# Cross-attention block on one Trainium2 core: denominators' sums over keys moved from TensorE to accumulating transfers and VectorE, the residual moved to transfers

## The chip, the cores and the metric

The kernel runs on one NeuronCore of a Trainium2 chip. The metric is device time in microseconds (us) for one execution, the median of a few runs; lower is better. All arithmetic is float32.

## The reference

Queries are 4096 rows of `x` (512 wide), keys and values come from 3202 rows of a context, there are 16 heads of 32. What matters, cut from the reference:

```python
xq  = _ada_ln(x_q,  t_vec, Wss_q,  bss_q)      # layer norm, then scale and shift from silu(t_vec)
xkv = _ada_ln(x_kv, t_vec, Wss_kv, bss_kv)
q  = (xq @ Wq + bq).reshape(B, Lq, nh, dh)
kv = (xkv @ Wkv + bkv).reshape(B, Lkv, 2, nh, dh)
k, v = kv[:, :, 0], kv[:, :, 1]
scores = jnp.einsum('bqhd,bkhd->bhqk', q, k) / jnp.sqrt(jnp.float32(dh))
attn = jax.nn.softmax(scores, axis=-1)
out = jnp.einsum('bhqk,bkhd->bqhd', attn, v).reshape(B, Lq, H)
return x_q + (out @ Wp + bp)
```

## The kernel before, in words

**Stages.** A first stage of about 230 us normalises the context, projects keys and values and stores them in DRAM; it also normalises the rows of `x` and projects the queries of the first block. Then comes the attention, on which all that follows bears. A check at the end (a flag computed from the largest denominator and reciprocal) can start an exact second pass; with these inputs it isn't taken.

**Units and tiles.** The 4096 queries are 8 blocks (`b`) of 512. The 16 heads are 4 groups (`g`) of 4 heads. One block with one group is a unit (`u = 4*b + g`, 32 units). Each unit goes over 25 tiles (`t`) of 128 keys; the last two keys of the 3202 are the "tail" and are treated apart. In a tile TensorE makes the scores of the next tile (`scores`, L1152, keys on the partitions), ScalarE takes exp of them in two instructions of 128x1024 (`weights`, L1411) into one of five buffers `pt`, and TensorE multiplies the values with them (`weigh`, L1164), accumulating in a PSUM bank over the unit. VectorE adds up the `pt` buffers (L1738): even and odd tiles go to two accumulators `acc` and `odd`, 23 additions of 128x2048 in a unit, and a 24th (L1747) joins the two. ScalarE may not write a `pt` buffer again before TensorE and VectorE have both read it, five tiles later.

**Side work.** TensorE has room for one small extra step behind `weigh` in each tile, written out by hand: `first_side` for `g == 0` and `later_side` for the others. The steps are parts of the query projection of the next block (L1184), of the output projection of the block before (L1222), the scores of the tail (L1207), and the denominators (`denominators`, L1195): in tiles 5 and 6 of a unit, TensorE multiplies the joined accumulator of the unit before with ones, which sums over the 128 partitions, that is over keys. All these results land in the one bank that isn't accumulating; ScalarE takes them out (`take_queries` L1420, `take_output` L1440, `take_denominators` L1427), and a `jobs` list orders them.

**From denominators to outputs.** SP (the engine that issues nearly all transfers, in program order, each behind its own waits) stores the denominators in DRAM (`store_l`, L771). Once per block it loads them, with the tail's weights, as a 128x64 tile (`load_l`, L799), VectorE adds and inverts them (`invert`, L1642 to L1649), SP stores the reciprocals and loads them back, each copied to 32 partitions (`store_r`, `load_r`), and VectorE multiplies (`divide`, L1671, four instructions of 128x512). The products feed the output projection. VectorE adds the bias to the rows of `x` (`add_bias`, L1678) and these to each output tile (`add_residual`, L1684); SP stores it (`store_y`, L832). The last unit alone sums its denominators by TensorE with the tail included, and turns them with VectorE transposes (L1754 to L1762).

**Other waits.** SP also loads the keys and values of the next unit in five parts (`load_kv`, L750 and L751, after `pv_done` of the same part), and the tail's weights copied to 32 partitions (`load_tail`, L788). POOL (GpSimd) does nothing in the attention. TensorE waits at a side step for `job_taken` of the job before (`free`), and at `denominators` for `p_added`.

Of the kernel before, what the change touches and what calls it, by code (L numbers as in the profile page):

```python
# [5 lines left out]
P = 128  # L6
F32 = mybir.dt.float32
I32 = mybir.dt.int32
ALU = mybir.AluOpType
# [7 lines left out]
NH = 16  # L17
# [4 lines left out]
def cross_attention(nc, x, ctx, cond, Wq, bq, Wkv, bkv, Wp, bp, Wss_q, bss_q, Wss_kv, bss_kv, out):  # L22
    _, LQ, H = x.shape
    LKV = ctx.shape[1]
    DH = H // NH
# [52 lines left out]
    def attention():  # L78
        with ExitStack() as st:
# [47 lines left out]
            l_blk = sb("l_blk", [P, QB * NH // P])  # L127
            l_t = sb("l_t", [P, 2, QB * NH // P])
            l_a = sb("l_a", [P, QB * NH // P])
            l_c = sb("l_c", [P, QB * NH // P])  # L130
            r_blk = sb("r_blk", [P, QB * NH // P])
            r_few = sb("r_few", [P, QB // DH])
            l_tops = sb("l_tops", [P, 2, NB + 1])
# [12 lines left out]
            acc = [part(5 + i).rearrange("p (h q) -> p h q", h=HG) for i in range(2)]  # L146
            odd = [part(i).rearrange("p (h q) -> p h q", h=HG) for i in (7, 12)]
            acc2 = odd[0]
            on = part(8).rearrange("p (g q) -> p g q", g=NG)
            r_b = part(9).rearrange("p (g q) -> p g q", g=NG)  # L150
            xy = [part(i).rearrange("p (j f) -> p j f", j=TPB) for i in (10, 13)]
# [55 lines left out]
            l_out = sem("l_out")  # L207
# [3 lines left out]
            l_in = sem("l_in")  # L211
            l_step = sem("l_step")
            r_done = sem("r_done")
            r_out = sem("r_out")
            r_in = sem("r_in")
            on_ready = sem("on_ready")
            xy_in = sem("xy_in")
            xy_ready = sem("xy_ready")
            y_added = sem("y_added")
            y_out = [sem(f"y_out{j}") for j in range(TPB)]  # L220
            turned = sem("turned")
# [64 lines left out]
            def schedule():  # L286
                jobs = []
                for b in range(NB):
                    for g in range(NG):
                        u = NG * b + g  # L290
                        if g == 0:
                            if b > 0:
                                jobs.append(("q", b, 3, 0))
                                jobs.append(("l", u - 1))
                                jobs.extend(("q", b, 3, i) for i in range(1, q_parts(3)))
                            jobs.append(("p", b))
                            if b > 0:
                                jobs.extend(("y", b - 1, 0, i) for i in range(2))
                        else:
                            if b > 0:  # L300
                                jobs.append(("y", b - 1, g, 0))
                            jobs.append(("l", u - 1))
                            if b > 0:
                                jobs.extend(("y", b - 1, g, i) for i in (1, 2))
                            if b + 1 < NB:
                                jobs.extend(("q", b + 1, g - 1, i) for i in range(2))
# [18 lines left out]
            def added(u):  # L325

                return ADDS * u
# [140 lines left out]
            def exact_pool(pool):  # L468
                for j in range(TPB):
                    pool.wait_ge(y_out[j], 16 * NB)  # L470
# [214 lines left out]
            with nc.Block() as block:  # L685
                @block.sync
                def _(sp):
# [80 lines left out]
                    def store_l(u):  # L768
                        b, g = divmod(u, NG)
                        sp.wait_ge(job_taken, JOB["l", u] + 1)  # L770
                        sp.dma_start(l_dram[g * HG:(g + 1) * HG, b * QB:(b + 1) * QB],  # L771
                                     l_sb[0:P:DH, :]).then_inc(l_out, 16)
# [18 lines left out]
                    def load_l(b, heads):  # L791

                        cols = slice(b * QB, (b + 1) * QB)
                        rows = heads * P // NH
                        sp.wait_ge(l_out, 16 * (NG * b + heads // HG))
                        sp.wait_ge(pt_out, 16 * NG * (b + 1))
                        if b > 0:
                            sp.wait_ge(l_step, 4 * b)
                        sp.dma_start(l_blk[0:rows, :], l_dram[0:heads, cols].rearrange("h (a q) -> h a q", a=P // NH)  # L799
                                     ).then_inc(l_in, 16)  # L800
                        for k in range(TAIL):
                            src = pt_dram[:, cols].rearrange("(h k) q -> k h q", k=TAIL)[k, 0:heads, :]
                            sp.dma_start(l_t[0:rows, k, :], src.rearrange("h (a q) -> h a q", a=P // NH)
                                         ).then_inc(l_in, 16)

                    def store_r(b, heads):
                        rows = heads * P // NH
                        sp.wait_ge(r_done, b + 1)
                        sp.dma_start(r_dram[0:heads, b * QB:(b + 1) * QB].rearrange("h (a q) -> h a q", a=P // NH),
                                     r_blk[0:rows, :]).then_inc(r_out, 16)  # L810

                    def load_r(b, heads):
                        groups = heads // HG
                        sp.wait_ge(r_out, 16 * (b + 1))
                        if b == 0:
                            sp.wait_ge(xs_out[4], 16)
                        if b > 0:
                            sp.wait_ge(on_ready, NG * b)
                        for h in range(HG):
# [992 lines left out]
```

## Time and profile before

| | |
|---|---|
| Median of 3 runs (lowest to highest) | 2140.96 us (2140.28 to 2142.82) |
| Profiled execution, its own time | 2138.16 us |
| Profiled execution, its span | 2136.4 us |
| Granted TensorE clock, mean | 0.999 of full speed |
| Busy share: TensorE / VectorE / ScalarE / GpSimd | 99% / 90% / 84% / 1% |
| DMA, mean rate over the span | 99 GB/s |

How to read it: PE is TensorE's matmuls, PEld its weight loads (which overlap PE), DVE VectorE, ACT ScalarE, POOL GpSimd, SP the engine that issues transfers. "L1164" is line 1164 of the kernel before. A float32 matmul shows as two records. Matmuls are pipelined and their ends are modelled, so the distance from one `weigh` to the next says more of a tile's length than busy time does. A timeline row gives start, duration, engine, line, operation, output and input, and a count if equal instructions are merged; a bracket is the idle time ahead and who ended it.

### The profile page before, as it was taken

What the parts mean: (1) busy time and instruction counts of PE and PEld (TensorE: products, weight loads), DVE (VectorE), ACT (ScalarE), POOL (GpSimd) and SP (SyncE); (2) the same over time, 40 slices, a digit from 0 to 9 for tenths busy, and PEclk for the clock granted to TensorE, in tenths of its full rate; (3) what the DMA queues carried; (4) which work ended last, traced back from release to release, by engine and by line L of the source; (5) the groups of instructions that cost most, each with busy time, mean ns of one, the idle gap of its engine ahead of it and who ended that gap; (6) DMA issues with size and microseconds to landing.
All of it is one profiled execution on the core that took longest, in us unless ns stands there. A gap on an engine that the chain in (4) does not pass through costs nothing.

```text
span 2136.4 us, 56258 instructions
## 1 busy us (share of the span) xinstructions
PE 2114.3 (99%) x25036; PEld 604.5 (28%) x25036; DVE 1923.6 (90%) x1197; ACT 1802.1 (84%) x1923; POOL 17.3 (1%) x28
## 2 busy tenths in 40 slices
PE   7999999999999999999999999999999999999998
PEld 3444322222222222222222222222222222222222
DVE  2435799999999999999999999999999999999998
ACT  1212799999999999999999999999999999999995
POOL 0001000000000000000000000000000000000000
PEclk9999999999999999999999999999999999999999
DMA  9346534223422343223422342223432332232321
GB/s 314 115 161 235 148 86 97 77 80 92 118 75 77 95 102 86 67 80 92 121 71 82 89 122 71 78 79 89 110 83 71 101 95 78 70 84 78 97 55 52
DMA packets 202260, 212.35 MB, mean 99 GB/s; under 512 B 18838, under 2 KB 136222, under 8 KB 202012
## 3 DMA queue, kind: packets, MB, share of 16 engines
q1 hardware_dynamic: 199468, 208.16, 35.1%
q8 instruction: 198, 3.24, 0.6%
q10 hardware_dynamic: 2544, 0.53, 0.1%
q14 instruction: 50, 0.41, 0.1%
HBM read 170.38 MB, written 38.26 MB: 98 GB/s over the span
## 4 chain that ended last, share of the span: by engine, by line
PE 98%; DVE 1%; DMA 0%; issue 0%; ACT 0%; POOL 0%; SPq 0%; DVEq 0%
PE bank L1152 40%; PE bank L1164 37%; PE bank L1222 5%; PE bank L1184 5%; PE bank L1056 4%; PE bank L1067 4%; PE bank L1195 1%; PE bank L1280 1%; PE bank L1036 0%; DVE stats L1507 0%; PE bank L1207 0%; DMA arena<-in_L_xcond_Wss_kv_dram 0%; DVE arena L1525 0%; PE bank L1001 0%; PE bank L1097 0%
## 5 line engine op out<-in xcount | busy, mean ns | idle before, releaser
L1411 ACT ACTIVATE arena<-bank,shift 128x1024 f32<-128x1024 f32 x1600 | 1692.5, 1114 | 132.9 <-PE bank L1152 131.4
L1738 DVE TENSOR_TENSOR arena<-arena 128x2048 f32<-128x2048 f32 x736 | 1641.3, 2283 | 60.7 <-ACT arena L1411 59.0
L1152 PE MATMUL bank<-qs,ks 32*64 32x512 f32 x12800 | 918.2, 613 | 1.2 <-ACT arena L1369 0.7
L1164 PE MATMUL bank<-arena,vg 128*32 128x512 f32 x6400 | 852.3, 605 | 1.2 <-ACT arena L1411 1.2
L1164 PEld LDWEIGHTS bank<-arena,vg 128*32 128x32 f32 x6400 | 125.9, 108 | 650.5 <-ACT arena L1411 650.5
L1152 PEld LDWEIGHTS bank<-qs,ks 32*64 32x64 f32 x12800 | 205.0, 129 | 366.4 <-ACT arena L1411 227.0
L1222 PE MATMUL bank<-wp,arena 128*32 128x168 f32 (+2 forms) x2464 | 153.6, 321 | 0.0
L1184 PE MATMUL bank<-xt,wq 128*32 128x256 f32 (+2 forms) x2016 | 143.0, 355 | 0.0
L1222 PEld LDWEIGHTS bank<-wp,arena 128*32 128x32 f32 x2464 | 80.1, 110 | 184.3 <-issue 165.4
L1369 ACT ACTIVATE arena<-bank,bk_c 128x512 f32<-128x512 f32 (+1 forms) x28 | 17.9, 642 | 128.6 <-PE bank L1056 120.5
L1184 PEld LDWEIGHTS bank<-xt,wq 128*32 128x32 f32 x2016 | 65.5, 110 | 150.8 <-issue 132.8
L1056 PE MATMUL bank<-arena 128*128 128x512 f32 (+1 forms) x224 | 90.8, 549 | 1.2 <-ACT arena L1346 1.2
L1067 PE MATMUL bank<-arena 128*128 128x512 f32 x200 | 90.2, 594 | 0.6 <-DVE arena L1587 0.6
L1587 DVE TENSOR_TENSOR arena<-bank,bv_b 128x512 f32<-128x512 f32 x25 | 16.9, 688 | 77.6 <-PE bank L1067 77.6
L1747 DVE TENSOR_TENSOR arena<-arena 128x2048 f32<-128x2048 f32 x32 | 73.4, 2292 | 1.1
L1056 PEld LDWEIGHTS bank<-arena 128*128 128x128 f32 x224 | 39.7, 190 | 44.6 <-issue 43.9
L1067 PEld LDWEIGHTS bank<-arena 128*128 128x128 f32 x200 | 37.7, 190 | 47.3 <-issue 45.7
L1525 DVE TENSOR_SCALAR arena<-arena,aggr,rstd 128x512 f32<-128x512 f32 x54 | 25.9, 542 | 20.8 <-POOL rstd L960 20.8
L1346 ACT ACTIVATE arena<-bank,mod 128x512 f32<-128x512 f32 (+1 forms) x28 | 18.6, 746 | 29.7 <-PE bank L1036 15.7
L1507 DVE BATCH_NORM_STATS2 stats<-arena 128x6 f32<-128x512 f32 x54 | 33.6, 680 | 6.2 <-DMA arena<-in_ctx_dram 6.1
L1195 PE MATMUL bank<-arena,ones 128*32 128x256 f32 x496 | 38.1, 379 | 0.0
L1671 DVE TENSOR_TENSOR arena<-o_all,arena 128x512 f32<-128x512 f32 x31 | 19.4, 686 | 11.2 <-DMA arena<-l_recip 11.2
(97 smaller groups left out, 384.9 us busy)
## 6 DMA issues: line engine op xcount, KB each, us to landing
ks<-k_full SPq DMA_DIRECT2D x160, 320.0 KB, 3.1
vg<-v_full SPq DMA_DIRECT2D x160, 320.0 KB, 3.8
p_b<-p_tails SPq DMA_DIRECT2D x128, 128.0 KB, 4.2
arena<-in_x_dram SPq DMA_DIRECT2D x15, 1024.0 KB, 9.8
q_full<-qs SPq DMA_DIRECT2D x32, 256.0 KB, 2.0
out_dram<-arena SPq DMA_DIRECT2D x32, 256.0 KB, 2.5
x_normal<-arena SPq DMA_DIRECT2D x7, 1024.0 KB, 7.6
xin<-x_normal SPq DMA_DIRECT2D x28, 256.0 KB, 10.1
```

The costliest lines, as they stand in the source:

```text
L1056: mm = nc.tensor.matmul(bank[:, 4 + 2 * (n % 2), 0:width], w[:, k, m * P:(m + 1) * P], src[:, k, 0:width], start=(k == 0), stop=(k == FT - 1))
L1067: mm = nc.tensor.matmul(bank[:, 5 + 2 * (n % 2), :], ct[c % 2][:, k, j * P:(j + 1) * P], wkv[:, k, H:2 * H], start=(k == 0), stop=(k == FT ...
L1152: mm = nc.tensor.matmul(bank[out, 2 * (i % RING) + h % 2, :], ks[rows_of(h), keys], qs[rows_of(h), g, :], start=True, stop=True)
L1164: mm = nc.tensor.matmul(bank[rows_of(h), o_bank(u), :], vg[:, t, rows_of(h)], pt[t % PR][:, h, :], start=(t == 0), stop=False, skip_group_ ...
L1184: mm = nc.tensor.matmul(bank[rows_of(c), side_bank(u), cols], wq[:, k, col:col + DH], xt[:, k, cols], start=(k == 0), stop=(k == FT - 1), ...
L1195: mm = nc.tensor.matmul(bank[rows_of(h), side_bank(u), halves_of(half)], ones[:, :], acc[of % 2][:, h, halves_of(half)], start=True, stop= ...
L1222: mm = nc.tensor.matmul(bank[rows_of(c), side_bank(u), cols], on[:, k, row:row + DH], wp[:, k, cols], start=(k == 0), stop=(k == NG - 1), ...
L1411: nc.scalar.activation(pt[t % PR][:, 2 * pair:2 * pair + 2, :], bank[:, first:first + 2, :], ACT.Exp, scale=SCALE, bias=shift[:, g:g + 1]) ...
L1507: i = nc.vector.bn_stats(stats[:, j, :], src[:, j, :])
L1525: return nc.vector.tensor_scalar(to, rows, aggr[:, j, 0:1], rstd[:, j:j + 1], ALU.subtract, ALU.mult)
L1738: nc.vector.tensor_tensor(a[:, :, :], (pt[t - 1] if k <= 2 else a)[:, :, :], pt[t % PR][:, :, :], ALU.add).then_inc(p_added, 1)
L1747: nc.vector.tensor_tensor(sums[0][:, :, :], sums[0][:, :, :], sums[1][:, :, :], ALU.add).then_inc(p_added, 1)
```

## The change

TensorE's `denominators`, ScalarE's `take_denominators` and VectorE's joining addition go, except for the last unit. In their place, for each unit but the last: SP copies partitions 0 to 31 of both accumulators into a tile `folds` whose rows belong to head `h` (`first_folds`, four transfers of 32 partitions x 2 rows of 2 KB), and POOL issues accumulating transfers that add partitions 32 to 63, 64 to 95 and 96 to 127 on top, then one that adds the tail's weights to one partition of each head (`fold`: four rounds of four; each transfer waits for the one before it of the same head). In the next unit, VectorE adds the two halves (`sum_folds`, behind the addition of tile 11), transposes in blocks of 32x32, reduces and inverts (`invert`), transposes back (`spread`) and multiplies (`divide`), four tiles in a row. The denominators and reciprocals no longer go through DRAM. An accumulator may be overwritten two units later, once its folds have landed.

The residual: for blocks 0 to 6 SP copies `x` to the output in DRAM (`copy_x`), POOL adds the bias by an accumulating transfer (`add_bias`, 1 MB) and then each output tile (`add_output`, 256 KB each). VectorE's `add_bias` and `add_residual` stay for the last block alone.

Side steps: output parts in tiles 1 to 12 (before 1 to 4 and 7 to 14), query parts in 14 to 21 (before 15 to 22); for `g == 0` query parts in 1 to 12, tail scores in 13 (before 15), outputs in 16 to 23 as before. The number of these steps and their columns stay.

The diff, cut to its core:

```diff
             def added(u):
-                return ADDS * u
+                return (ADDS - 1) * u
+            FOLDS = P // DH
...
-                    def store_l(u):
...
+                    def first_folds(u):
+                        sp.wait_ge(p_added, added(u + 1))
+                        if u == 0:
+                            sp.wait_ge(xs_out[4], 16)
+                        else:
+                            sp.wait_ge(l_step, 5 * (u - 1) + 2)
+                        for h in range(HG):
+                            sp.dma_start(folds[rows_of(h), :, :], both[u % 2][0:DH, :, h, :]).then_inc(fold_in, 16)
...
+                    def copy_x(b):
+                        sp.dma_start(out2[b * QB:(b + 1) * QB, :], x2[b * QB:(b + 1) * QB, :]).then_inc(x_copied[b % 2], 16)
...
                             if u > 0:
                                 load_kv(u, NC - 1)
+                                first_folds(u - 1)
                             if more:
                                 load_kv(u + 1, 0)
-                            if g == 1 and b > 0:
-                                store_y(b - 1, 0)
-                            if u > 0:
-                                store_l(u - 1)
...
+                    def add_output(b, j):
+                        if j == 0:
+                            pool.wait_ge(b_added[b % 2], 16 * (b // 2 + 1))
+                        pool.wait_ge(job_taken, JOB[y_last(b, j)] + 1)
+                        pool.dma_start(out2[b * QB + j * P:b * QB + (j + 1) * P, :], y_sb[:, j, :],
+                                       accum_op=ALU.add).then_inc(y_out[j], 16)
+
+                    def fold(u):
+                        b, g = divmod(u, NG)
+                        for s in range(1, FOLDS + 1):
+                            for h in range(HG):
+                                if s == 1:
+                                    pool.wait_ge(fold_in, 16 * HG * (u + 1))
+                                else:
+                                    pool.wait_ge(folded[h], 16 * (FOLDS * u + s - 1))
+                                if s < FOLDS:
+                                    pool.dma_start(folds[rows_of(h), :, :], both[u % 2][s * DH:(s + 1) * DH, :, h, :],
+                                                   accum_op=ALU.add).then_inc(folded[h], 16)
+                                else:
+                                    if h == 0:
+                                        pool.wait_ge(pt_out, 16 * NG * (b + 1))
+                                    row = (g * HG + h) * TAIL
+                                    pool.dma_start(folds[h * DH:h * DH + 1, :, :],
+                                                   pt_dram[row:row + TAIL, b * QB:(b + 1) * QB].unsqueeze(0),
+                                                   accum_op=ALU.add).then_inc(folded[h], 16)
+
+                    for u in range(1, UNITS):
+                        b, g = divmod(u, NG)
+                        fold(u - 1)
+                        if b > 0 and g == 0:
+                            add_bias(b - 1)
+                        if b > 0:
+                            add_output(b - 1, g)
...
+                        if b > 0 and 1 <= t < 13:
+                            project_queries(u, b, 3, (t - 1) // FT, (t - 1) % FT)
+                        if t == 13:
                             tail_scores(u, b)
+                        if b > 0 and 16 <= t < 24:
+                            output(u, b - 1, 0, (t - 16) // NG, (t - 16) % NG)
...
+                        if b > 0 and 1 <= t < 13:
+                            output(u, b - 1, g, (t - 1) // NG, (t - 1) % NG)
+                        if b + 1 < NB and 14 <= t < 22:
+                            project_queries(u, b + 1, g - 1, (t - 14) // FT, (t - 14) % FT)
...
+                    def sum_folds(v):
+                        for h in range(HG):
+                            dve.wait_ge(folded[h], 16 * FOLDS * (v + 1))
+                        nc.vector.tensor_tensor(folds[:, 0, :], folds[:, 0, :], folds[:, 1, :], ALU.add).then_inc(l_step, 1)
+                        dve.wait_ge(l_step, 5 * v + 1)
+                        nc.vector.transpose(blocks(l_sb[:, :]), blocks(folds[:, 0, :])).then_inc(l_step, 1)
+
+                    def invert(v):
+                        some = slice(v * QB // DH, (v + 1) * QB // DH)
+                        dve.wait_ge(l_step, 5 * v + 2)
+                        nc.vector.tensor_reduce(l_keep[:, some], blocks(l_sb[:, :]), op=ALU.add, axis=AX_X).then_inc(l_step, 1)
+                        dve.wait_ge(l_step, 5 * v + 3)
+                        nc.vector.reciprocal(r_keep[:, some], l_keep[:, some]).then_inc(l_step, 1)
+
+                    def spread(v):
...
+                        if u > 0:
+                            if t == 11:
+                                sum_folds(u - 1)
+                            if t == 12:
+                                invert(u - 1)
+                            if t == 13:
+                                spread(u - 1)
+                            if t == 14:
+                                divide(u - 1)
...
                             if k == 1 and u >= 2:
-                                dve.wait_ge(job_done, DONE["l", u - 2] + 1)
...
+                                for h in range(HG):
+                                    dve.wait_ge(folded[h], 16 * FOLDS * (u - 1))
...
-                        dve.wait_ge(p_added, added(u) + ADDS - 1)
-                        nc.vector.tensor_tensor(sums[0][:, :, :], sums[0][:, :, :], sums[1][:, :, :], ALU.add
-                                                ).then_inc(p_added, 1)
...
+                    dve.wait_ge(p_added, added(UNITS))
+                    nc.vector.tensor_tensor(sums[0][:, :, :], sums[0][:, :, :], sums[1][:, :, :], ALU.add
+                                            ).then_inc(p_added, 1)
```

## Rows read from the trace of the kernel before

**Rows 1.** Page, part 1 (busy time, share, instructions) and the granted clock by slice.

```profile
PE 2114.3 (99%) x25036; PEld 604.5 (28%) x25036; DVE 1923.6 (90%) x1197; ACT 1802.1 (84%) x1923; POOL 17.3 (1%) x28
...
PEclk9999999999999999999999999999999999999999
```

**Rows 2.** Page, part 4: the chain that ended last, by engine.

```profile
PE 98%; DVE 1%; DMA 0%; issue 0%; ACT 0%; POOL 0%; SPq 0%; DVEq 0%
```

**Rows 3.** Busy time by engine, one unit (block 1, group 2): PE, PEld, DVE, ACT, POOL, clock, DMA.

```profile
574.30:633.60 59.30, 59.30 (x785) 15.83 (x777) 57.65 (x29) 54.96 (x59) 0.00 (x0) 1.00 0.27 75
```

**Rows 4.** Timeline, TensorE: the two denominator tiles of that unit, `weigh` rows.

```profile
585.95 1.06 PE L1164 MATMUL bank<-arena,vg 128*32 128x512 f32 x8
...
588.42 1.07 PE L1164 MATMUL bank<-arena,vg 128*32 128x512 f32 x8
...
590.89 1.06 PE L1164 MATMUL bank<-arena,vg 128*32 128x512 f32 x8
```

**Rows 5.** Timeline, TensorE: `weigh` of tiles 24 and 0, without side work, and of 1.

```profile
572.25 1.06 PE L1164 MATMUL bank<-arena,vg 128*32 128x512 f32 x8
...
574.29 1.06 PE L1164 MATMUL bank<-arena,vg 128*32 128x512 f32 x8
...
576.59 0.64 PE L1164 MATMUL bank<-arena,vg 128*32 128x512 f32 x4
```

**Rows 6.** Groups by line and shape, ScalarE and VectorE (busy us, mean ns | idle before).

```profile
L1411 ACT ACTIVATE arena<-bank,shift 128x1024 f32<-128x1024 f32 x1600 | 1692.5, 1114 | 132.9 <-PE bank L1152 131.4
L1662 DVE SCALAR_TENSOR_TENSOR o_all<-p_b,vt,bss_b 128x512 f32<-128x512 f32 x32 | 23.8, 744 | 0.0
L1693 DVE STREAM_TRANSPOSE xt<-xin 128x2048 f32<-128x2048 f32 x7 | 16.1, 2303 | 0.0
L1601 DVE TENSOR_REDUCE s_max<-bank 128x1 f32<-128x512 f32 x4 | 2.5, 683 | 4.9 <-PE bank L1089 4.9
L1754 DVE STREAM_TRANSPOSE arena<-l_sb 128x512 f32<-128x512 f32 x1 | 0.7, 711 | 1.3 <-ACT l_sb L1427 1.3
L1762 DVE TENSOR_TENSOR arena<-o_all,r_sb 128x512 f32<-128x512 f32 x1 | 0.7, 693 | 0.0
L1756 DVE RECIPROCAL r_few<-arena 128x16 f32<-128x16 f32 x1 | 0.3, 254 | 0.0
```

**Rows 7.** Timeline, VectorE: last addition of a unit, joining addition; seven additions later.

```profile
572.77 2.28 DVE L1738 TENSOR_TENSOR arena<-arena 128x2048 f32<-128x2048 f32 x1
575.08 2.29 DVE L1747 TENSOR_TENSOR arena<-arena 128x2048 f32<-128x2048 f32 x1
...
602.35 15.49 DVE L1738 TENSOR_TENSOR arena<-arena 128x2048 f32<-128x2048 f32 x7
```

**Rows 8.** Timeline, SP: key and value load at a unit's end; four `p_b` transfers.

```profile
573.38 0.33 SPq L750 DMA_DIRECT2D ks<-k_full  x1
573.75 0.44 SPq L751 DMA_DIRECT2D vg<-v_full  x1
...
609.20 1.89 SPq L788 DMA_DIRECT2D p_b<-p_tails  x4
```

**Rows 9.** Page, part 6: transfers, KB each, median us from issue to landing.

```profile
p_b<-p_tails SPq DMA_DIRECT2D x128, 128.0 KB, 4.2
...
q_full<-qs SPq DMA_DIRECT2D x32, 256.0 KB, 2.0
out_dram<-arena SPq DMA_DIRECT2D x32, 256.0 KB, 2.5
...
xin<-x_normal SPq DMA_DIRECT2D x28, 256.0 KB, 10.1
```

**Rows 10.** Groups by line, POOL: the longest of its instructions.

```profile
L960 POOL TENSOR_TENSOR rstd<-var_eps,minus_half 128x4 f32<-128x4 f32 x15 | 15.2, 1013 | 192.2 <-DVE var_eps L1518 184.7 <-issue 7.5
```

**Rows 11.** Timeline at the end: output matmuls of the last block, the last joining addition.

```profile
2112.93 7.13 PE L1280 MATMUL bank<-wp,arena 128*128 128x512 f32 x16
...
2118.07 2.29 DVE L1747 TENSOR_TENSOR arena<-arena 128x2048 f32<-128x2048 f32 x1
```

More of the change, by code:

```diff
@@ L145, in attention @@
             pt = [part(i).rearrange("p (h q) -> p h q", h=HG) for i in range(PR)]
-            acc = [part(5 + i).rearrange("p (h q) -> p h q", h=HG) for i in range(2)]
-            odd = [part(i).rearrange("p (h q) -> p h q", h=HG) for i in (7, 12)]
+            acc = [part(5 + 2 * i).rearrange("p (h q) -> p h q", h=HG) for i in range(2)]
+            odd = [part(6 + 2 * i).rearrange("p (h q) -> p h q", h=HG) for i in range(2)]
             acc2 = odd[0]
-            on = part(8).rearrange("p (g q) -> p g q", g=NG)
-            r_b = part(9).rearrange("p (g q) -> p g q", g=NG)
-            xy = [part(i).rearrange("p (j f) -> p j f", j=TPB) for i in (10, 13)]
+            both = [arena[:, (5 + 2 * i) * W:(7 + 2 * i) * W].rearrange("p (a h q) -> p a h q", a=2, h=HG) for i in range(2)]
+            on = [part(i).rearrange("p (g q) -> p g q", g=NG) for i in (12, 10)]
+            folds = part(9)[:, 0:2 * QB].rearrange("p (a q) -> p a q", a=2)
+            l_keep = part(9)[:, 2 * QB:3 * QB]
+            r_keep = part(9)[:, 3 * QB:4 * QB]
+            blocks = lambda rows: rows.rearrange("p (c j) -> p c j", j=DH)
+            xy = part(13).rearrange("p (j f) -> p j f", j=TPB)
             y_sb = part(11).rearrange("p (j f) -> p j f", j=TPB)
@@ L210, in attention @@
             tail_added = sem("tail_added")
-            l_in = sem("l_in")
+            fold_in = sem("fold_in")
+            folded = [sem(f"folded{h}") for h in range(HG)]
             l_step = sem("l_step")
-            r_done = sem("r_done")
-            r_out = sem("r_out")
-            r_in = sem("r_in")
+            last_step = sem("last_step")
             on_ready = sem("on_ready")
+            x_copied = [sem(f"x_copied{i}") for i in range(2)]
+            b_added = [sem(f"b_added{i}") for i in range(2)]
             xy_in = sem("xy_in")
@@ L220, in attention @@
             y_out = [sem(f"y_out{j}") for j in range(TPB)]
+            last_out = [sem(f"last_out{j}") for j in range(TPB)]
             turned = sem("turned")
@@ L806, in store_r @@
[L806 to L819, printed above, removed]
-                            src = r_dram[0:heads, b * QB:(b + 1) * QB].rearrange("(g j) q -> j g q", j=HG)[h:h + 1, :, :]
-                            sp.dma_start(r_b[rows_of(h), 0:groups, :],
-                                         src.broadcast_to([DH, groups, QB])).then_inc(r_in, 16)
@@ new lines, in divide @@
+                    def divide(v):
+                        b, g = divmod(v, NG)
+                        dve.wait_ge(l_step, 5 * v + 5)
+                        dve.wait_ge(tail_added, TAIL * (v + 1))
+                        if v == 0:
+                            dve.wait_ge(v_out[0], 16 * ((KB + 1) // 2 + HG))
+                        if v == NG:
+                            dve.wait_ge(k_out[0], 16 * ((KB + 1) // 2))
+                        if b > 1 and g == 0:
+                            dve.wait_ge(job_done, DONE[y_last(b - 2, TPB - 1)] + 1)
+                        nc.vector.tensor_tensor(on[b % 2][:, g, :], o_all[:, g, :], r_sb[:, :], ALU.mult).then_inc(on_ready, 1)
@@ L1676, in add_bias, with range_so_far @@
+                    def range_so_far():
+                        some = slice(0, (UNITS - 1) * QB // DH)
+                        nc.vector.reduce_max(l_tops[:, 0, 0:1], l_keep[:, some], AX_X).then_inc(last_step, 1)
+                        nc.vector.reduce_max(l_tops[:, 1, 0:1], r_keep[:, some], AX_X).then_inc(last_step, 1)
+                    def add_bias():
+                        dve.wait_ge(xy_in, 16)
                         dve.wait_ge(bp_in, 16)
-                        rows = xy[b % 2]
```

261 lines of the change are left out of this document (66 added, 195 removed).

## The prediction, made before the changed kernel was run

> **What bounds the kernel now.** I read the busy times first, then the chain, then single units. TensorE is busy 99% of the span at full granted clock [rows 1], and the chain that ended last is 98% TensorE [rows 2]. So only TensorE's own work, or something that makes TensorE wait, can move the time. The windows view says how near the next engines are: in a unit of 59.3 us TensorE has no gap, VectorE is busy 57.65 and ScalarE 54.96 [rows 3]. VectorE is 1.7 us behind the bound, so each microsecond put on it counts almost at once.
>
> **The change part by part.**
>
> *Denominators leave TensorE.* In each of 31 units, two tiles that carried a denominator step become empty. A tile with that step lasts 588.42 - 585.95 = 2.47 us, and the next one the same [rows 4]. Empty tiles come at 2.04 and 2.30 in turn, 574.29 - 572.25 and 576.59 - 574.29 [rows 5], 2.17 on average. What TensorE's tile then costs is set with ScalarE beside it, whose two exps take 1.06 each when they follow closely (54.96 us of a unit, some 53 of it exps; one alone is listed at 1.114 [rows 3, 6]), so 2.17 can't fall much. Best case per unit: 2 x (2.47 - 2.17) = 0.60. Worst case, where each new empty tile is one of the 2.30 kind: 0.34. For the 28 units with side work around I take the middle, 0.47, which makes 13.2. The three units 1 to 3 of block 0 have a long run of empty tiles around, and the tile behind the pair is relieved too: 0.75 each, 2.2. Together 15.4 us, with ends of 10.5 and 19.
>
> *Query parts and outputs shift by a tile or two.* Same steps, same columns, so no cost; the takes by ScalarE keep their distance of one tile behind the last part. ScalarE loses one 128x512 take per unit, which lies beside TensorE.
>
> *VectorE.* It loses the joining addition (2.29 in the row, 2.21 of pitch, since additions in a row come every 15.49/7 = 2.213 us [rows 7]), residual additions and the bias addition, all but the last block's. It gains per unit an addition of 128x512 (0.69), two transposes (0.71 each), a reduction (0.68) and a small reciprocal (0.25); the multiplication (0.69) it had [rows 6]. I sum the new load: 23 x 2.213 = 50.9, two tail additions 1.5, these six 3.7, together 56.1 us; with the turn of queries (2.30 [rows 6]) in group 0, 58.4. The new TensorE unit is 59.3 - 0.5 = 58.8. VectorE stays hidden, by 2.7 us in three units of four and by under 1 us in the fourth.
>
> *The fold chain* is the part that decides. From VectorE's last addition of a unit to `sum_folds` behind tile 11 of the next, five rounds of four transfers run one behind the other: one from SP, four from POOL. VectorE's own loop closes through it: chain C, then 3.7 for the six instructions, then 13 additions x 2.213 = 28.8, then the next chain; plus 2.30/4 for the turn. So a unit can't be shorter than C + 33.1, and TensorE's 58.8 holds as long as C is below 25.7 us. What is queued behind a late fold on VectorE is the addition of tile 12; behind that ScalarE, which waits for `pt` buffers, and then TensorE.
>
> C has to be bounded, since the trace before has no accumulating transfer and none issued by POOL. The first round: SP issues four transfers of the same shape, 32 partitions x two rows of 2 KB, in 1.89 us, 0.47 each [rows 8], and `p_b` lands 4.2 after its issue [rows 9], behind a key and value load just as here [rows 8]: 1.9 + 4.2 = 6.1. A POOL round takes the longer of four issues and one issue plus landing. Issue: from below SP's 0.47; from above one addition of VectorE, 2.2, if POOL should have to wait for it. POOL's one long instruction is 1.01 [rows 10], the nearest row, and I take 1.0. Landing: from below 2.0 for 256 KB out of SBUF, from above 10.1 for `xin` [rows 9]. Nearest are the plain transfers out of SBUF with 2 KB rows and nothing queued ahead, 2.0 and 2.5; I take 2.5. Then a round is 4.0, and C = 6.1 + 3 x 4.0 + (4.0 + 2.5) = 24.6. That is hidden by 1.1 us. The low ends give 6.1 + 3 x 2.5 + 3.9 = 17.5, the high ends 6.1 + 3 x 12.3 + 18.9 = 61.9, which would cost 31 x 36 = 1120 us.
>
> *SP.* Four folds are issued between two loads; the next load waits for tile 4 of the unit, over 8 us later, so nothing behind them is late unless VectorE lags several tiles. SP loses the stores of denominators, the loads of reciprocals and the output stores. *POOL* is empty in the attention, but in order: `add_output` of group 0 waits for the last take of its unit (tile 24), ahead of the next fold; its issue is over before SP's round has landed. In groups 1 to 3 it waits for tile 13, behind the fold. The 1 MB transfers (`copy_x`, `add_bias`) fall in the middle of a unit, beside no fold round but at most the last; their cover is the block that follows. I cost these at nothing; if an accumulate into DRAM slows the first POOL round, that is a microsecond in 7 units.
>
> *The end.* The last block's first output matmuls run from 2112.93 to 2120.06, and the joining addition ends at 2120.36 [rows 11], so VectorE is late by 0.3 us at most there; that is all a lighter VectorE can give.
>
> **Sum.** The profiled execution took 2138.16 (span 2136.4): 2138.2 - 15.4 = 2122.8. The median of the runs lies 2.8 higher, so I forecast 2125.5, in figures 2125.
>
> **The rivals.**
>
> *Late folds (slower).* Place: VectorE's wait in `sum_folds`. It decides from C = 25.7; from 26.2 the saving is eaten. For it: only 1.1 us of room, and an accumulating transfer has to read its destination as well, so its landing may be that of `p_b`, 4.2, and not 2.5. Then a round is 5.2, C = 6.1 + 15.6 + 8.2 = 29.9, and 31 x 4.2 = 130 us come on top: 2255. With a landing of 3.6 it is C = 27.5 and 2181. Against it: 4.2 was measured behind 640 KB of keys and values, which the POOL rounds mostly are not. Chance 0.24, half of it up to 2181. The Trainium skill's "Collectives: The Full Stack", section "The bandwidth ceiling: the fold count and why AG ≠ RS ≠ AR", says that a reducing transfer reads two sources and so runs at about half the rate of a copy; no row here shows one. By that rule, taken on all of the 2.5 us, landing would be 5.0, C 33.1 and the estimate 2354.
>
> *POOL's issue held up by VectorE (much slower).* If POOL can only issue when VectorE is between two instructions, an issue takes up to an addition, 2.2, and a round 8.8: C = 6.1 + 3 x 8.8 + 8.8 + 2.5 = 43.8, and 31 x 18.1 = 561 us make it 2686. For it: VectorE is busy without a gap for seven additions in a row [rows 7]. Against: nothing in the trace shows POOL and VectorE at work together, so it is open. Chance 0.05. The Trainium skill's "SBUF — State Buffer", section "Summary: rules for kernel authors", says that transfers issued from GpSimd starve in making their descriptors while VectorE runs in its two-port modes. These additions, 2048 elements in 2.28 us, go at one element per cycle, so by the page's condition it should not bite.
>
> *Nothing gained.* The chain costs just what the tiles give (C from 25.8 to 26.3), or the empty tiles stay near 2.47 because ScalarE or VectorE paces them. Time 2137 to 2145. Rows 5 speak against the second. Chance 0.07. That the change doesn't do what it says is no rival here: the steps are gone from the code. Only "in two halves" says little, since the query parts were so cut before.
>
> **How the numbers follow.** The forecast has 0.64 (its own range 2118 to 2131, from the ends 10.5 and 19 and the spread of the runs). With late folds at 0.24, held-up issue 0.05 and nothing gained 0.07 that makes faster 0.64, same 0.07, slower 0.29, where "same" is within 0.2%, 4.3 us, about what a measurement of this kernel can tell from no change. The range goes from 2112, for an empty tile a little better than in the rows, to 2185, which takes in nothing gained and the half of late folds with landings up to 3.6: 0.64 + 0.07 + 0.12.
>
> **What would show it.** Right: denominators gone from TensorE's rows, unit pitch 58.7 to 59.0, the first new VectorE addition of 128x512 idle by less than 1 us with no transfer as releaser, POOL's issues near 1 us, the fourth round landing about 25 us after the last addition. Wrong: idle time of that addition released by an accumulating transfer, ScalarE's exps waiting for VectorE's additions, and unit pitch equal to C + 33; or empty tiles still at 2.4.

## The result, and the profile after

The changed kernel took 2154.2 us (median of 4 runs, 2152.64 to 2156.8), the kernel before beside it 2140.62: a ratio of 1.0064, 95% interval 1.005 to 1.0077. It is slower by 13.6 us where 15 us faster was forecast; the case that came true is the first rival, late folds.

The page of the changed kernel first: busy times with the granted clock, and the chain that ended last.

```profile
PE 2125.0 (99%) x24540; PEld 609.6 (28%) x24540; DVE 1888.4 (88%) x1247; ACT 1786.3 (83%) x1892; POOL 469.3 (22%) x559
...
PEclk9999999999999999999999999999999999999999
...
PE 69%; issue 11%; DMA 10%; DVE 6%; POOL 2%; SPq 1%; ACT 1%; DVEq 0%; ACTq 0%; POOLq 0%
```

TensorE still shows as 99% busy, as in [rows 1]; VectorE and ScalarE have less work than before, and only POOL has more. On busy time alone the kernel looks as TensorE-bound as ever. The chain tells otherwise: in [rows 2] it was TensorE for 98% of the span, here for 69%, and transfers, VectorE and POOL hold 18% between them. (A matmul's busy time is modelled: the scores' matmuls are listed with 956.7 us here and 918.2 before for the same 12800 records, so a short stall hides inside "busy".)

The waits view of the changed kernel says who waits (engine, output and line, releaser: us in all, times, longest):

```profile
DVE arena L1605 <- DMA arena<-p_tails: 109.9, 31, 5.7
...
ACT arena L1381 <- DVE arena L1686: 40.7, 59, 1.6
```

L1605 is `sum_folds`. VectorE waits there in each of the 31 units, 3.5 us on average, and the releaser is the last accumulating round, the tail's weights. ScalarE (L1381, the exps) then waits for VectorE's additions (L1686), which it never did before. One chain from the timelines of SP, POOL and VectorE, for the folds of block 2, group 1, read in the next unit:

```profile
819.02 1.89 SPq L772 DMA_DIRECT2D arena<-arena  x3
...
824.01 3.49 POOL L963 DMA_DIRECT2D arena<-arena  x4 [38.88 <-DMA arena<-arena]
830.23 5.15 POOL L963 DMA_DIRECT2D arena<-arena  x6 [2.73 <-DMA arena<-arena]
835.92 0.83 POOL L963 DMA_DIRECT2D arena<-arena  x1 [0.54 <-DMA arena<-arena]
837.61 0.83 POOL L963 DMA_DIRECT2D arena<-arena  x1 [0.85 <-DMA arena<-arena]
838.88 0.82 POOL L969 DMA_DIRECT2D arena<-p_tails  x1 [0.44 <-DMA arena<-arena]
...
843.01 0.79 POOL L969 DMA_DIRECT2D arena<-p_tails  x1 [0.64 <-DMA arena<-arena]
...
826.84 11.10 DVE L1686 TENSOR_TENSOR arena<-arena 128x2048 f32<-128x2048 f32 x5
837.85 4.49 DVE L1686 TENSOR_TENSOR arena<-arena 128x2048 f32<-128x2048 f32 x2
846.91 0.69 DVE L1605 TENSOR_TENSOR arena<-arena 128x512 f32<-128x512 f32 x1 [4.57 <-DMA arena<-p_tails]
...
856.86 26.51 DVE L1686 TENSOR_TENSOR arena<-arena 128x2048 f32<-128x2048 f32 x12
```

SP starts at 819.02, POOL's first issue follows 5.0 us later, the tail's round is issued from 838.88 to 843.80, and VectorE goes on at 846.91: C = 27.9 us here. Over the 31 units C is 27.0 on average (25.2 to 29.0). (The rows at 846.91 and 856.86 are 9.95 us apart. Between them lie the six small instructions and three additions, so the six add 3.3 us; ten more additions complete the loop.) What follows on ScalarE and TensorE in the same unit:

```profile
853.67 2.12 ACT L1381 ACTIVATE arena<-bank,shift 128x1024 f32<-128x1024 f32 x2 [0.91 <-DVE arena L1686]
...
856.46 2.12 ACT L1381 ACTIVATE arena<-bank,shift 128x1024 f32<-128x1024 f32 x2 [0.30 <-DVE arena L1686]
...
850.53 1.07 PE L1164 MATMUL bank<-arena,vg 128*32 128x512 f32 x8
853.00 1.06 PE L1164 MATMUL bank<-arena,vg 128*32 128x512 f32 x8
855.86 1.07 PE L1164 MATMUL bank<-arena,vg 128*32 128x512 f32 x8
858.64 1.07 PE L1164 MATMUL bank<-arena,vg 128*32 128x512 f32 x8
861.45 1.07 PE L1164 MATMUL bank<-arena,vg 128*32 128x512 f32 x8
```

The first two `weigh` starts are 2.47 us apart, a query tile as it should be; the next three tiles take 2.86, 2.78 and 2.81. That is where the time goes: a few tiles behind `sum_folds`, here three, stretched by some 0.35 us each. The transfers (KB each, median us from issue to landing) point to the cause:

```profile
ks<-k_full SPq DMA_DIRECT2D x160, 320.0 KB, 3.5
vg<-v_full SPq DMA_DIRECT2D x160, 320.0 KB, 5.2
arena<-arena POOLq DMA_DIRECT2D x372, 128.0 KB, 5.2
...
arena<-arena SPq DMA_DIRECT2D x124, 128.0 KB, 2.4
```

An accumulating transfer of 128 KB lands 5.2 us after its issue; SP's plain copy of the same shape takes 2.4.

### The profile page after: what moved, and what is told of

It reads as the page before. It is cut to its first block, busy times and chain, and to the rows that moved or that the text cites. A ratio compares the mean times of both kernels' runs of the same rounds, so it can differ in the third digit from the quotient of the medians.

```text
span 2153.1 us, 55853 instructions
## 1 busy us (share of the span) xinstructions
PE 2125.0 (99%) x24540; PEld 609.6 (28%) x24540; DVE 1888.4 (88%) x1247; ACT 1786.3 (83%) x1892; POOL 469.3 (22%) x559
## 4 chain that ended last, share of the span: by engine, by line
PE 69%; issue 11%; DMA 10%; DVE 6%; POOL 2%; SPq 1%; ACT 1%; DVEq 0%; ACTq 0%; POOLq 0%
PE bank L1152 28%; PE bank L1164 25%; DMA arena<-arena 8%; PE bank L1056 4%; DVE arena L1686 4%; PE bank L1067 4%; PE bank L1211 3%; PE bank L1184 3%; POOL arena L963 2%; DMA arena<-p_tails 1%; SPq L772 1%; PE bank L1250 1%; PE bank L1036 0%; ACT arena L1381 0%; DMA arena<-in_L_xcond_Wss_kv_dram 0%
## 5 line engine op out<-in xcount | busy, mean ns | idle before, releaser
L1381 ACT ACTIVATE arena<-bank,shift 128x1024 f32<-128x1024 f32 x1600 | 1690.5, 1113 | 160.0 <-PE bank L1152 114.7
L1686 DVE TENSOR_TENSOR arena<-arena 128x2048 f32<-128x2048 f32 x736 | 1633.5, 2280 | 10.9 <-ACT arena L1381 10.9
L1152 PE MATMUL bank<-qs,ks 32*64 32x512 f32 x12800 | 956.7, 613 | 1.5 <-ACT arena L1381 0.7
L963 POOL DMA_DIRECT2D arena<-arena x372 | 319.0, 1158 | 1138.4 <-DMA arena<-arena 1128.1
L1152 PEld LDWEIGHTS bank<-qs,ks 32*64 32x64 f32 x12800 | 225.6, 130 | 410.6 <-issue 210.4
L969 POOL DMA_DIRECT2D arena<-p_tails x124 | 101.3, 851 | 96.6 <-DMA arena<-arena 94.4
L1605 DVE TENSOR_TENSOR arena<-arena 128x512 f32<-128x512 f32 x31 | 21.5, 692 | 109.9 <-DMA arena<-p_tails 109.9
L951 POOL DMA_DIRECT2D out_dram<-arena x28 | 30.1, 1074 | 191.4 <-ACT arena L1408 191.0
L920 POOL TENSOR_TENSOR rstd<-var_eps,minus_half 128x4 f32<-128x4 f32 x15 | 15.2, 1013 | 192.7 <-DVE var_eps L1470 185.9
## 6 DMA issues: line engine op xcount, KB each, us to landing
arena<-in_x_dram SPq DMA_DIRECT2D x8, 1024.0 KB, 10.1
```

The lines of the kernel that those rows point to most:

```text
L951: pool.dma_start(out2[b * QB + j * P:b * QB + (j + 1) * P, :], y_sb[:, j, :], accum_op=ALU.add).then_inc(y_out[j], 16)
L963: pool.dma_start(folds[rows_of(h), :, :], both[u % 2][s * DH:(s + 1) * DH, :, h, :], accum_op=ALU.add).then_inc(folded[h], 16)
L969: pool.dma_start(folds[h * DH:h * DH + 1, :, :], pt_dram[row:row + TAIL, b * QB:(b + 1) * QB].unsqueeze(0), accum_op=ALU.add).then_inc(fol ...
L1152: mm = nc.tensor.matmul(bank[out, 2 * (i % RING) + h % 2, :], ks[rows_of(h), keys], qs[rows_of(h), g, :], start=True, stop=True)
L1381: nc.scalar.activation(pt[t % PR][:, 2 * pair:2 * pair + 2, :], bank[:, first:first + 2, :], ACT.Exp, scale=SCALE, bias=shift[:, g:g + 1]) ...
L1686: nc.vector.tensor_tensor(a[:, :, :], (pt[t - 1] if k <= 2 else a)[:, :, :], pt[t % PR][:, :, :], ALU.add).then_inc(p_added, 1)
```

## The experiments

**Moving VectorE's steps.** Runs late, mid and early change nothing but the tile behind which `sum_folds` and its three successors stand. The diff of late; mid has 12 to 15, early 9 to 12:

```diff
-                            if t == 11:
+                            if t == 14:
                                 sum_folds(u - 1)
-                            if t == 12:
+                            if t == 15:
                                 invert(u - 1)
-                            if t == 13:
+                            if t == 16:
                                 spread(u - 1)
-                            if t == 14:
+                            if t == 17:
                                 divide(u - 1)
```

Expected of late: 

> VectorE's four steps on the folds stand three tiles later (14 to 17 in place of 11 to 14), nothing else is changed. Theory 1, the fold chain ends too late for VectorE (C is 27.0 us on average in the changed kernel, and a unit can't be shorter than C plus the VectorE work behind it): three additions fewer stand behind the wait, so the loop allows C up to 32; the wait of the first fold addition falls from 109.9 us in all to under 10, ScalarE's waits for additions from 40.7 us to near 0, and the time is 2127 us (2123 to 2131), below both kernels. Theory 2, the loss comes from what the transfers do elsewhere (slower loads, contention, empty tiles that save nothing): the time stays between 2145 and 2156.

Measured: 2128.66 us (2128.09 to 2130.88), ratio to the kernel before 0.9949 (0.9936 to 0.9963). The group of `sum_folds` in run late (busy us, mean ns | idle before):

```profile
L1605 DVE TENSOR_TENSOR arena<-arena 128x512 f32<-128x512 f32 x31 | 21.2, 684 | 0.0
```

No wait is left, and the exps wait for no addition. Three tiles' delay of four small instructions turns 13.6 us of loss into 11.3 of gain. Theory 2 falls: the same transfers run, the last of them lands 27.1 us after SP's start (26.8 in the changed kernel), and the time is back at what TensorE needs. The chain that ended last is again TensorE for 98%.

Expected of mid: 

> VectorE's four steps one tile later than in the changed kernel (12 to 15). Theory 1: the loop allows C up to 27.9 us, and C was 25.2 to 29.0, 27.0 on average, so about a quarter of the units wait by some tenths: 2129 to 2136 us. Without theory 1 (run late's gain would come from some other effect of the later place): in the middle between 2154 and 2129, some 2146.

Measured: 2132.14 us (2131.03 to 2133.5), ratio 0.996 (0.9945 to 0.9975). VectorE waits for folds in 11 units, 18.9 us in all:

```profile
DVE arena L1605 <- DMA arena<-p_tails: 18.9, 11, 2.9
```

The time lies in the range of theory 1, but not for its reason. The 11 waits are 1.7 us on average and not some tenths, and still the units are as long as in run late (58.94 us in groups 1 to 3 of blocks 1 to 6), so up to the last one VectorE makes up for what it waits. Only at the end does its lateness show: TensorE waits longer for the last denominators in run mid (second row) than in run late (first row), and its matmuls there run at the lower of its two clocks, 1.2 GHz (granted clock 0.51 from 2110.4 to 2113.8), 1.90 us for 1.07.

```profile
2111.08 1.07 PE L1263 MATMUL bank<-arena,ones 128*32 128x512 f32 x8 [1.38 <-issue]
...
2110.36 1.90 PE L1263 MATMUL bank<-arena,ones 128*32 128x512 f32 x8 [3.02 <-issue]
```

Differences of 1 to 3 us among the runs near 2130 say little by themselves: the first stage alone takes 227.3 to 230.7 us in the ten traces.

Expected of early: 

> The same four steps two tiles earlier (9 to 12). Theory 1: two more additions stand behind the wait, the loop is C + 33.1 + 4.4 = 64.5 us against 58.9 of TensorE, so 31 x 5.6 = 174 us come on top of 2127: 2300 us (2270 to 2330), and the wait of the first fold addition grows to 6 to 8 us per unit. Theory 2: within 10 us of the changed kernel.

Measured: 2306.64 us (2303.7 to 2313.97), ratio 1.0775 (1.0758 to 1.0791); the same group in run early:

```profile
L1605 DVE TENSOR_TENSOR arena<-arena 128x512 f32<-128x512 f32 x31 | 21.5, 692 | 262.1 <-DMA arena<-p_tails 262.1
```

The wait is 8.5 us per unit, a little over the 6 to 8 expected. TensorE's granted clock was 0.971 on average here (0.998 in run late), for short stretches at its lower level of 1.2 GHz. The loop accounts for the units without it: C, 27.7, and VectorE's work behind it, 36.5 (38.6 with the turn of queries), make the 64.6 us that a unit takes on average from the second on, where run late has 58.7. Four places now stand in one order: steps from tile 9 give 2306.6, from 11 2154.2, from 12 2132.1, from 14 2128.7. This is what a loop through the chain does: a place with slack is free, and once the slack is gone each tile earlier costs about one addition's time in every unit (two tiles, from 11 to 9, cost 4.9 us a unit; two additions are 4.4, and C is 0.7 longer).

**Shortening the chain at the old place.** Run notail leaves out POOL's fourth round:

```diff
-            FOLDS = P // DH
+            FOLDS = P // DH - 1
...
-                                if s < FOLDS:
+                                if True:
```

Expected: 

> The fourth POOL round, which adds the tail's weights to the denominators, is left out, so the denominators miss two keys of 3202; VectorE's steps stay at tiles 11 to 14. Theory 1: the chain loses its last round, about 6 us, C falls to 20 to 22, VectorE no longer waits, and the time is 2127 us (2123 to 2131). Theory 2: 2145 to 2156, since only 4 KB transfers are gone.

Measured: 2129.57 us (2129.29 to 2131.09), ratio 0.9954 (0.9939 to 0.9969). POOL's last issue ends 20.0 us after SP's first on average, in the changed kernel 25.1. But the last landing, which ends the chain, comes after 24.4 us in place of 26.8: the chain is shorter by 2.4 us and not by some 6, and C did not fall to the 20 to 22 expected. Nor are the waits of `sum_folds` all gone; 11.3 us in 8 units are left, and they cost nothing, as in run mid. So it is the length of the chain against the place of its reader, and neither VectorE's place nor the tail's transfers as such.

**Why landing takes 5.2 us.** Run plain lets POOL copy in its three rounds in place of adding, so the denominators are wrong by what is overwritten:

```diff
-                                    pool.dma_start(folds[rows_of(h), :, :], both[u % 2][s * DH:(s + 1) * DH, :, h, :],
-                                                   accum_op=ALU.add).then_inc(folded[h], 16)
+                                    pool.dma_start(folds[rows_of(h), :, :], both[u % 2][s * DH:(s + 1) * DH, :, h, :]).then_inc(folded[h], 16)
```

Expected: 

> POOL's three rounds of 128 KB copy in place of adding, so the denominators hold the last quarter of the partitions and the tail alone; same bytes out of the accumulators, same issuing engine, same order. If the landing of 5.2 us comes from the accumulate itself (it has to read the destination too), it falls to 2.4 to 3.2 us, the landing of the plain copies that SP issues, C falls to about 21 and the time to 2127 us (2123 to 2131). If it comes from POOL's way of issuing or from key and value loads under way, landing stays at 4.5 to 5.2 us and the time at 2145 to 2156.

Measured: 2132.27 us (2130.01 to 2132.94), ratio 0.9962 (0.995 to 0.9974), no wait of VectorE for a fold. Its transfers, and POOL's groups (busy us in all):

```profile
arena<-arena POOLq DMA_DIRECT2D x372, 128.0 KB, 3.0
```

```profile
L963 POOL DMA_DIRECT2D arena<-arena x372 | 201.2, 547 | 1104.6 <-DMA arena<-arena 1087.7 <-issue 14.3
```

The same bytes out of the accumulators, from the same engine in the same order, land in 3.0 us as copies and in 5.2 as additions. The record of an issue is shorter too, 0.55 us on average against 0.83 for one that stands alone in the changed kernel. But in a row the records overlap, and issues start some 0.55 us apart in both kernels.

The time is 1.3 us above the 2123 to 2131 expected, and the chain ends after 23.3 us where about 21 was expected. The units are as long as in run late; what is longer is POOL's closing DRAIN, on which the program's end waits (9.9 us in place of 7.8; see "The end" below).

Run quiet keeps the additions and takes other traffic away: SP holds back the unit's first two loads of keys and values until the folds have landed.

```diff
+                            if u > 0:
+                                for h in range(HG):
+                                    sp.wait_ge(folded[h], 16 * FOLDS * u)
                             if more:
                                 load_kv(u + 1, 0)
```

Expected: 

> The changed kernel with VectorE's steps where they are, but SP issues the first two key and value loads of a unit only when the folds have landed (they are needed some 30 us later), so the fold rounds have the DMA engines more to themselves. If these loads are a part of the landing of 5.2 us (copies of the same shape issued by POOL beside them took 3.0), it falls to 3.5 to 4.5 us, C to 23 to 25.5, and the time to 2128 to 2134. If the accumulate alone sets it, landing stays above 4.9 and the time above 2147.

Measured: 2129.36 us (2128.01 to 2130.29), ratio 0.9946 (0.9931 to 0.9961). The fold transfers land in

```profile
arena<-arena POOLq DMA_DIRECT2D x372, 128.0 KB, 4.2
```

and the chain ends after 24.0 us in place of 26.8; VectorE waits 1.1 us in all. So about 1 of the 5.2 us was the key and value loads, of which one starts beside POOL's first round and one beside its third. In the changed kernel these two rounds land in 5.7 and 5.8 us (medians), the second in 3.5. That share was enough to decide the sign.

The comparison of 3.0 with 5.2 is not like for like, because in run plain the loads fall beside other rounds. The traces settle it: with no key or value load in flight, the transfers land in 4.2 us when they add (all 372 of run quiet) and in 2.4 when they copy (101 of the 372 in run plain). Of the 2.7 us by which the landing exceeds the forecast 2.5, adding thus makes some 1.8 and the loads 1.0.

**The residual alone.** Run res_only is the kernel before with the residual by transfers (SP copies `x` to the output, POOL adds bias and output tiles, VectorE's `add_residual` goes and its `add_bias` stays for the last block), denominators still on TensorE. The core of its edit:

```diff
-                            if g == 1:
+                            if g == 1 and b == NB - 1:
                                 load_xy(b)
+                            if g == 1 and b < NB - 1:
+                                copy_x(b)
...
+                    for u in range(NG, UNITS):
+                        b, g = divmod(u, NG)
+                        if g == 0:
+                            add_bias(b - 1)
+                        add_output(b - 1, g)
...
-                        if b > 0 and t == (3 if g == 1 else 17):
-                            add_residual(b - 1, 0 if g == 1 else g)
-                        if b > 0 and g == 1 and t == 17:
-                            add_residual(b - 1, 1)
```

Expected: 

> The kernel before with the residual alone moved to transfers (copy of x, bias and output tiles added by accumulating transfers from POOL); denominators stay on TensorE. Theory 1 (TensorE is the bound, VectorE and the transfers are hidden): no change, 2137 to 2142 us. Rival: the accumulates into DRAM slow the loads or hold up the output tiles' buffer: 2145 or more. Other rival: VectorE's relief of some 37 us over the program shortens it: 2130 to 2136; then part of run late's gain is the residual's.

Measured: 2140.39 us (2138.32 to 2142.88), ratio 1.0001 (0.9992 to 1.001). No change: the residual's share in gain and loss is nil while TensorE is the bound.

**The empty tiles' place.** Run late13 is run late with the query parts one tile earlier, so that tile 13 is no longer empty between outputs and queries:

```diff
-                        if b + 1 < NB and 14 <= t < 22:
-                            project_queries(u, b + 1, g - 1, (t - 14) // FT, (t - 14) % FT)
+                        if b + 1 < NB and 13 <= t < 21:
+                            project_queries(u, b + 1, g - 1, (t - 13) // FT, (t - 13) % FT)
...
-                                if b + 1 < NB and t in (18, 22):
-                                    take_queries(u, b + 1, g - 1, (t - 18) // FT)
+                                if b + 1 < NB and t in (17, 21):
+                                    take_queries(u, b + 1, g - 1, (t - 17) // FT)
```

Expected: 

> The kernel of run late, and the query parts one tile earlier still (13 to 20, taken at 17 and 21), so that the empty tile 13 joins the run of empty tiles at the end of a unit. From run late's tiles: an empty tile that stands alone lasts 2.30 us, a run of four (22, 23, 24, 0) 8.92. If a run of five lasts 10.96 (2.30, 2.04, 2.30, 2.04, 2.28), 0.26 us are saved in each of 21 units: 5 us below run late, near 2124. If what counts is the number of empty tiles and not their place, the time stays within 1 us of 2129.

Measured: 2125.03 us (2122.13 to 2125.42), ratio 0.9923 (0.991 to 0.9937): the fastest kernel of the study, ahead of both. The empty tiles 21 to 24 and 0 of one unit in run late13 (TensorE's timeline, `weigh` rows):

```profile
1034.45 1.06 PE L1164 MATMUL bank<-arena,vg 128*32 128x512 f32 x8
1036.75 1.06 PE L1164 MATMUL bank<-arena,vg 128*32 128x512 f32 x8
1038.79 1.06 PE L1164 MATMUL bank<-arena,vg 128*32 128x512 f32 x8
1041.09 1.06 PE L1164 MATMUL bank<-arena,vg 128*32 128x512 f32 x8
1043.13 1.06 PE L1164 MATMUL bank<-arena,vg 128*32 128x512 f32 x8
1045.43 1.06 PE L1164 MATMUL bank<-arena,vg 128*32 128x512 f32 x8
```

2.30, 2.04, 2.30, 2.04, 2.30: every second tile of a run is the short one. In run late, with tile 13 apart, a lone empty tile goes from 605.29 to 607.59:

```profile
605.29 1.07 PE L1164 MATMUL bank<-arena,vg 128*32 128x512 f32 x8
607.59 1.07 PE L1164 MATMUL bank<-arena,vg 128*32 128x512 f32 x8
```

2.30 us, hardly less than the 2.33 of a tile with an output part.

## Why the prediction was wrong, point by point

**The bound** was read rightly: TensorE first, VectorE just behind. The VectorE loop was right in form. Its size was 0.5 us too large: behind the wait VectorE works 32.05 us in a unit and 34.25 with the turn of queries, 32.6 on average and not 33.1, since the six instructions add 3.3 us and not the sum of their listed durations, 3.7. So the threshold is 26.2 and not 25.7. With it the changed kernel should lose 31 x (27.0 - 26.2) = 25 us against run late, an estimate; 2154.2 - 2128.7 = 25.5 was measured. It is an average: TensorE's units are 57.0 us in block 0 and 56.3 in the last block, so their thresholds are lower, near 25 and 24. Run early lies 178 us above run late, where 174 was expected; that it came so near is partly luck, since C was 0.7 longer than assumed and the work behind it 0.5 shorter.

**The step that failed** is the one in "C has to be bounded": "Nearest are the plain transfers out of SBUF with 2 KB rows and nothing queued ahead, 2.0 and 2.5; I take 2.5." An accumulating transfer lands in 5.2, so the chain is 27.0 and not 24.6 us, on the other side of the threshold. In terms of the sum: the first round took 4.7 (6.1 forecast); the three accumulating rounds run from +4.7 to about +19.4, 4.9 each (4.0 forecast); the last round with its landing took 7.6 (6.5 forecast). The copy rows were the wrong nearest rows: adding costs 1.8 us of landing (4.2 against 2.4), and 1.0 is the loads'. The forecast argued that the POOL rounds mostly don't lie behind keys and values. The trace before already has two loads inside the 24.6 us after a unit's last addition, which ends at 575.05 [rows 7]:

```profile
584.73 0.33 SPq L750 DMA_DIRECT2D ks<-k_full  x1
...
596.66 0.33 SPq L750 DMA_DIRECT2D ks<-k_full  x1
```

The range of landing, 2.0 to 10.1, did hold the truth, and so did the range of the time; but with a threshold 1.1 us away, the middle of so wide a bound could not carry a chance of 0.64.

**The rival of late folds** had its mechanism, place and sign right, its price too high (2181 to 2255 for landings of 3.6 to 4.2, where 5.2 gave 2154). The traces show three reasons. The listed landing runs from the start of the issue, and a head's next transfer starts 0.28 us after its last one has landed (median), so "one issue plus landing" counts the issue twice, 1.0 us in each of three rounds. The first round took 4.7 and not 6.1. And the threshold is 26.2. By the forecast's formula a landing of 5.2 makes C = 33.9; it was 27.0. The Trainium skill's "Collectives: The Full Stack" ("The bandwidth ceiling: the fold count and why AG ≠ RS ≠ AR") says that a reducing transfer reads two sources and runs at half a copy's rate; 4.2 us against 2.4 with no loads beside agree with the direction. The 5.0 us that the prediction worked out from it for the landing meets the 5.2 only because the loads add 1.0, and its time, 2354, is 200 us too high.

**POOL held up by VectorE** did not happen: in the chain above six issues fall in 5.15 us from 830.23 on, inside five additions of VectorE without a gap (826.84 to 837.94). The rule in the Trainium skill's "SBUF — State Buffer" ("Summary: rules for kernel authors") has descriptors from GpSimd starve while VectorE is in its two-port modes; that nothing stalled beside these additions, which the prediction read as outside those modes, agrees with it.

**The saving on TensorE** was mis-sized as well, by the place of the tiles. The middle between ends was taken for what a new empty tile costs; but in run late tile 13 stands alone at 2.30 and the run of four makes 8.92, so a unit of groups 1 to 3 goes from 59.3 to 58.95, the low end, while one of group 0 goes from 60.16 to 59.55, the high end. Over all units the traces of the kernel before and of run late differ by 13.2 us, and by 18.5 with run late13, which joins the tiles; 15.4 was forecast.

**The end** was costed at nothing, with a gain of 0.3 us at most, and costs 3.1 in run late. TensorE waits 1.38 us for the last denominators (the first row under run mid above) where it waited 0.41 before, and the program ends 8.0 us after VectorE's last addition in place of 5.9, because POOL's closing DRAIN is still under way. The kernel before, then run late (a DRAIN row gives ns, shortest, median and longest, and its start in us):

```profile
2120.47 1.06 PE L1293 MATMUL bank<-arena,ones 128*32 128x512 f32 x8 [0.41 <-issue]
L685 POOLq DRAIN  x1: 123/123/123, 2130.7 to 2130.7; - x1
...
L682 POOLq DRAIN  x1: 7826/7826/7826, 2121.1 to 2121.1; - x1
```

That DRAIN takes 0.1 us where POOL has issued no transfer, 2.9 after 35 (run res_only), 7.7 after 407 (run notail) and 7.8 after 531 (run late); run plain's 9.9 shows that the number is not all. What sets it was not tried. So the medians of run late and the kernel before differ by 11.3 us, and that run late13 lies 15.5 below the kernel before, just the forecast saving of 15.4, is luck: a larger saving and a cost that was left out.

**Costed at nothing and rightly so:** the residual (run res_only, 1.0001) and SP's queue (no engine waits for a load of keys or values in the changed kernel). The shift of the query parts was costed at nothing too; as to its last tile that was wrong by 3.6 us (runs late and late13).

## What to carry to other kernels

When work leaves the bound engine for a chain of small transfers, write down the loop that this chain closes, and compare its slack with the uncertainty of one transfer's landing times the number of rounds; if the slack is smaller, put the reader later, which cost nothing here (run late) because the result is due later still. An accumulating transfer is not a copy: here it took 1.7 times a copy's landing, and twice with loads in its rounds, so look for loads that start there. A listed landing already holds the issue. And a busy share of 99% can hide stalls: the chain and the releasers of waits show them.

## What the runs showed of the hardware that was not expected

Adding in place of copying costs 1.8 us in the landing of a 128 KB transfer within SBUF: 4.2 us against 2.4 with no key or value load in flight (runs quiet and plain). Keys and values land later beside it too, `vg` in 5.2 us against 3.8 in the kernel before, and in 4.4 in run plain. POOL's closing DRAIN took 7.8 us after 531 transfers and 0.1 after none. Empty tiles on TensorE alternate between 2.30 and 2.04 us by their place in a run, so a single step taken away between two others gives back only 0.03 us behind a narrow step (2.33 to 2.30), and two neighbours give back the rest.
